# Windowed attention: the mask added by a matmul, maxima of two heads at once, exponentials read from PSUM

## What is computed

```python
def local_attention(q, k, v):
    w = n // WINDOW                                  # 8 windows
    bq = q.reshape(b, h, w, WINDOW, d) * QK_SCALE    # 8.0
    bk, bv = look_around(bk), look_around(bv)        # the window before and the own one: 256 keys
    sim = jnp.einsum('bhwid,bhwjd->bhwij', bq, bk)
    mask = (i < j) | (i > j + WINDOW) | (j == -1)
    sim = jnp.where(mask, -jnp.finfo(sim.dtype).max, sim)
    attn = jax.nn.softmax(sim, axis=-1)
    out = jnp.einsum('bhwij,bhwjd->bhwid', attn, bv)
```

## Time and profile before

| | |
|---|---|
| median of 3 runs | 1829.39 us (1828.5 to 1833.63) |
| the profiled execution | 1827.51 us, span 1825.5 us |
| TensorE busy | 1616.9 us (89%) |
| VectorE busy | 1272.9 us (70%) |
| ScalarE busy | 862.0 us (47%) |
| GpSimd busy | 425.2 us (23%) |
| mean granted TensorE clock | 0.938 of full speed |

### The profile page before, as it was taken

How to read it: one execution, slowest core, us unless ns; L and a number is a source line. 1 busy time by engine, 2 the same in 40 slices (tenths; PEclk the granted TensorE clock), 3 DMA queues, 4 the chain that set the end, 5 groups by cost and what they waited for, 6 DMA issues and landing times. The chain is left out here.

```text
span 1825.5 us, 27251 instructions
## 1 busy us (share of the span) xinstructions
PE 1616.9 (89%) x8733; PEld 1025.5 (56%) x8733; DVE 1272.9 (70%) x2366; ACT 862.0 (47%) x1584; POOL 425.2 (23%) x258
## 2 busy tenths in 40 slices
PE   6899999999987989898986898898699888888698
PEld 2512222222234878787874765775477765665476
DVE  3588988888876565757574683693777693693776
ACT  3305666666632514242422673674533674574442
POOL 2130000000015020202022372272322372263133
PEclk8958999999989989898988999999799999999799
DMA  5812222222200330303005000000100200000010
GB/s 179 152 18 36 36 36 36 37 36 36 36 21 20 97 116 0 115 0 115 0 0 195 28 2 1 0 0 0 46 1 14 61 2 1 0 0 0 23 47 23
DMA packets 59892, 71.56 MB, mean 39 GB/s; under 512 B 15234, under 2 KB 43794, under 8 KB 59796
## 3 DMA queue, kind: packets, MB, share of 16 engines
q1 hardware_dynamic: 58708, 66.98, 15.3%
q10 hardware_dynamic: 1088, 3.41, 0.5%
HBM read 59.66 MB, written 10.49 MB: 38 GB/s over the span
## 5 line engine op out<-in xcount | busy, mean ns | idle before, releaser
L557 DVE TENSOR_REDUCE a_mx<-bank 128x1 f32<-128x512 f32 x592 | 366.8, 685 | 43.5 <-PE bank L608 43.2
L543 ACT ACTIVATE a_pt<-bank 128x1024 f32<-128x1024 f32 x256 | 247.7, 1021 | 173.2 <-PE bank L655 173.2
L608 PE MATMUL bank<-ka,qa 96*128 96x512 bf16 x592 | 219.4, 415 | 5.9 <-PEq L163 2.1
L1803 PE MATMUL bank<-m_hn,m_w 128*128 128x512 f32 x576 | 151.4, 420 | 18.4 <-DVE m_hn L1934 16.4
L1346 PE MATMUL bank<-wqkv,w_hst 128*128 128x512 f32 x576 | 143.0, 411 | 17.3 <-DVE w_hst L1553 17.3
L655 PE MATMUL bank<-qa,ka 99*128 99x512 bf16 x512 | 153.4, 383 | 3.1 <-issue 3.1
L1317 POOL TENSOR_TENSOR w_sm<-w_sm,w_st 128x1024 f32<-128x1024 f32 (+1 forms) x64 | 133.2, 2093 | 86.9 <-DVE w_st L1594 86.9
L608 PEld LDWEIGHTS bank<-ka,qa 96*128 96x128 bf16 x592 | 48.9, 98 | 182.4 <-DVE a_mx L557 144.6
L986 PE MATMUL bank<-f_y,f_ET 128*128 128x256 f32 x768 | 120.8, 308 | 31.2 <-DVE f_y L1091 20.4
L1392 PE MATMUL bank<-w_kT,w_qz 128*128 128x256 f32 (+1 forms) x512 | 127.8, 386 | 18.8 <-DVE w_st L1587 8.8
L1803 PEld LDWEIGHTS bank<-m_hn,m_w 128*128 128x128 f32 x576 | 112.2, 195 | 55.8 <-issue 27.4
(11 more groups left out here) (239 smaller groups left out, 2728.8 us busy)
## 6 DMA issues: line engine op xcount, KB each, us to landing
f_wex<-in_W SPq DMA_DIRECT2D x8, 2048.0 KB, 12.0
qa<-qk_parts SPq DMA_DIRECT2D x66, 128.0 KB, 4.6
ka<-qk_parts SPq DMA_DIRECT2D x66, 128.0 KB, 6.9
qk_parts<-p_parts SPq DMA_DIRECT2D x16, 384.0 KB, 2.6
wqkv_raw<-in_wqkv SPq DMA_DIRECT2D x2, 1536.0 KB, 8.5
w<-in_w SPq DMA_DIRECT2D x2, 1536.0 KB, 8.7
phi<-in_phi SPq DMA_DIRECT2D x5, 512.0 KB, 3.6
p_xT<-in_xT ACTq DMA_DIRECT2D x2, 1024.0 KB, 9.9
```

Source lines behind the costliest of these rows:

```text
L543: nc.scalar.activation(pt[n % 2][:, 2 * ab:2 * ab + 2, :].rearrange("p h t -> p (h t)"), PB[ab][:, :], ACT.Exp, scale=HD0 ** -0.5).then_in ...
L557: V.reduce_max(mx[par][:, u // 2, u % 2:u % 2 + 1], mbank(u), X).then_inc(max_done, 1)
L608: mm(mbank(u), qa[slot][0:KS, h, it * P:(it + 1) * P], ka[slot][0:KS, h, jh * HALF:(jh + 1) * HALF], start=True, stop=True).then_inc(max_p ...
L1803: last = mm(PB[2 + f % 2][:, part * HALF:(part + 1) * HALF], w1s[cw][:, k, col + f * P:col + (f + 1) * P], hns[ch][:, hf, k, :], start=(n ...
```

## The change

The mask and the identity are kept in bf16 as well; GpSimd makes the copies. A matmul of the bf16 identity with the mask, broadcast over two heads, writes the mask into the PSUM of a pair of heads, and the two score matmuls add to it. The factor 8 goes into the copy of the queries. VectorE takes the negated maximum of two heads in one instruction that reads PSUM alone. The exponentials read the scores from PSUM and write sm. Semaphores count pairs: `s_ps`, `s_max` (in place of `s_masked`) and `e_done`. TensorE now waits for `e_done` where it waited for `s_masked`, and for `zeroed` at 6 instead of 4 a layer.

```diff
+        maskb, identb = sb("maskb", [P, 2 * WIN], BF16), sb("identb", [P, P], BF16)
...
+        def pair_of_heads(w, h):
+
+            c0 = (h % 4) * 2 * WIN
+            return PB[1 + h // 4][:, c0:c0 + 4 * WIN].rearrange("p (e n) -> p e n", e=2)[:, :, keys(w)]
...
-                pool.wait_ge(zeroed, 4 * (l + 1))
+                pool.wait_ge(zeroed, 6 * l + 4)
                 pool.wait_ge(ld_tab, 16 * 4 * (l + 1))
                 pool.wait_ge(G["ld_tab"], 32)
+                V.tensor_copy(maskb[:, :], mask[:, :]).then_inc(zeroed, 1)
+                V.tensor_copy(identb[:, :], ident[:, :]).then_inc(zeroed, 1)
...
                 pe.wait_ge(G["wqkv_high"], KD * (l + 1))
-                pe.wait_ge(zeroed, 4 * (l + 1))
+                pe.wait_ge(zeroed, 6 * (l + 1))
...
                         for h in heads:
-                            if h % 2 == 0 and w >= 1:
-                                pe.wait_ge(s_masked, H1 * (NW * b + w - 1) + h + 2)
+                            n = keys(w).stop - keys(w).start
+                            if h % 2 == 0:
+                                if w >= 1:
+                                    pe.wait_ge(e_done, HP * (NW * b + w - 1) + h // 2 + 1)
+                                mm(pair_of_heads(w, h), identb[:, :], maskb[:, keys(w)].unsqueeze(1).to_broadcast([P, 2, n]),
+                                   start=True, stop=False)
                             c0 = (h % 4) * 2 * WIN + keys(w).start
-                            n = keys(w).stop - keys(w).start
-                            mm(PB[1 + h // 4][:, c0:c0 + n], qz[:, w % 2, h // 2, h % 2, :],
-                               kT[:, h // 2, k0:k0 + n], start=True, stop=True).then_inc(s_ps, 1)
+                            last = mm(PB[1 + h // 4][:, c0:c0 + n], qz[:, w % 2, h // 2, h % 2, :],
+                                      kT[:, h // 2, k0:k0 + n], start=False, stop=(h % 2 == 1))
+                            if h % 2 == 1:
+                                last.then_inc(s_ps, 1)
...
-                            pe.wait_ge(s_masked, H1 * (NW * b + min(i, NW)))
+                            pe.wait_ge(e_done, HP * (NW * b + min(i, NW)))
...
                         for h in hs:
+                            if h == 0 and w >= 2:
+                                act.wait_ge(pt_ps, HP * (NW * b + w - 1))
                             if h % 2 == 0:
-                                act.wait_ge(s_masked, H1 * (NW * b + w) + h + 2)
-                            last = S(sm[:, w % 2, h, keys(w)], sm[:, w % 2, h, keys(w)], ACT.Exp,
-                                     bias=st[:, w % 2, 1, h:h + 1], scale=-1.0, accum_out=st[:, w % 2, 2, h:h + 1])
-                            if h % 4 == 3:
+                                act.wait_ge(s_max, HP * (NW * b + w) + h // 2 + 1)
+                            last = S(sm[:, w % 2, h, keys(w)], pair_of_heads(w, h - h % 2)[:, h % 2, :], ACT.Exp,
+                                     bias=st[:, w % 2, 1, h:h + 1], accum_out=st[:, w % 2, 2, h:h + 1])
+                            if h % 2 == 1:
                                 last.then_inc(e_done, 1)
...
-                                     PB[0][64 * e:64 * e + 64, 0:HALF].rearrange("p (a t) -> p a t", a=HP), ACT.Copy)
+                                     PB[0][64 * e:64 * e + 64, 0:HALF].rearrange("p (a t) -> p a t", a=HP), ACT.Copy,
+                                     scale=QK_SCALE)
...
                     def maxima(w, heads):
-                        s = w % 2
-                        if w >= 2:
-                            dve.wait_ge(pt_ps, HP * (NW * b + w - 1))
                         for h in heads:
-                            if h % 2 == 0:
-                                dve.wait_ge(s_ps, H1 * (NW * b + w) + h + 2)
-                                dve.sem_inc(passed, 1)
-                            c0 = (h % 4) * 2 * WIN
-                            V.tensor_tensor_reduce(sm[:, s, h, keys(w)], PB[1 + h // 4][:, c0:c0 + 2 * WIN][:, keys(w)],
-                                                   mask[:, keys(w)], -QK_SCALE, HIGHEST, ALU.add, ALU.min,
-                                                   st[:, s, 1, h:h + 1]).then_inc(s_masked, 1)
+                            dve.wait_ge(s_ps, HP * (NW * b + w) + h // 2 + 1)
+                            dve.sem_inc(passed, 1)
+                            if h == 0 and w >= 2:
+                                dve.wait_ge(e_done, HP * (NW * b + w - 1))
+                            V.tensor_reduce(st[:, w % 2, 1, h:h + 2], pair_of_heads(w, h), X, ALU.max,
+                                            negate=True).then_inc(s_max, 1)
```

More of the change, by code:

```diff
@@ L1265, in stage_attention1 @@
             "ld_tab", "tabs", "zeroed", "h_high", "h_low", "qk_ps", "v_ps", "qk_sb", "v_sb", "sq_done", "ss_done", "n_sqrt", "n_step"))
-        (qn_done, cos_done, sin_done, turn_done, tq_ps, tk_ps, qz_done, kT_done, s_ps, s_masked, e_done,
+        (qn_done, cos_done, sin_done, turn_done, tq_ps, tk_ps, qz_done, kT_done, s_ps, s_max, e_done,
          d_done, p_done, pt_ps, pt_act, pt_dve, pv_ps, oT_done, wo_ps, wo_done) = (sem(n) for n in (
-            "qn_done", "cos_done", "sin_done", "turn_done", "tq_ps", "tk_ps", "qz_done", "kT_done", "s_ps", "s_masked",
+            "qn_done", "cos_done", "sin_done", "turn_done", "tq_ps", "tk_ps", "qz_done", "kT_done", "s_ps", "s_max",
             "e_done", "d_done", "p_done", "pt_ps", "pt_act", "pt_dve", "pv_ps", "oT_done", "wo_ps", "wo_done"))
@@ L1578, in maxima @@
                     def maxima(w, heads):
-                        s = w % 2
-                        if w >= 2:
-                            dve.wait_ge(pt_ps, HP * (NW * b + w - 1))
                         for h in heads:
-                            if h % 2 == 0:
-                                dve.wait_ge(s_ps, H1 * (NW * b + w) + h + 2)
-                                dve.sem_inc(passed, 1)
-                            c0 = (h % 4) * 2 * WIN
-                            V.tensor_tensor_reduce(sm[:, s, h, keys(w)], PB[1 + h // 4][:, c0:c0 + 2 * WIN][:, keys(w)],
-                                                   mask[:, keys(w)], -QK_SCALE, HIGHEST, ALU.add, ALU.min,
-                                                   st[:, s, 1, h:h + 1]).then_inc(s_masked, 1)
+                            dve.wait_ge(s_ps, HP * (NW * b + w) + h // 2 + 1)
[4 more added lines that the diff above has]
+                                            negate=True).then_inc(s_max, 1)
                     def inverse_sums(w, j):
                         hs = slice(4 * j, 4 * j + 4)
-                        dve.wait_ge(e_done, 2 * (NW * b + w) + j + 1)
+                        dve.wait_ge(e_done, HP * (NW * b + w) + 2 * j + 2)
                         V.reciprocal(st[:, w % 2, 3, hs], st[:, w % 2, 2, hs]).then_inc(d_done, 1)
@@ L1629, in _ @@
                         if 1 <= i <= NW:
-                            maxima(i - 1, range(2))
+                            maxima(i - 1, (0,))
                         if i >= 2:
@@ L1633, in _ @@
                         if 1 <= i <= NW:
-                            maxima(i - 1, range(2, H1 - 2))
+                            maxima(i - 1, (2, 4))
                         if i >= 2:
@@ L1645, in _ @@
                         if 1 <= i <= NW:
-                            maxima(i - 1, range(H1 - 2, H1))
+                            maxima(i - 1, (6,))
                         if i < NW - 2:
```

## The result

The changed kernel takes 1841.77 us (median of 7 executions, 1839.83 to 1847.83) against 1828.5 us (7 executions, 1827.47 to 1833.63) before: a ratio of 1.0078, 95% interval 1.0059 to 1.0097. It is slower, by 13 to 14 us. The forecast was slower, 1855.7 us with a range from 1841 to 1868: the sign is right, the loss is half of what I worked out, and the time is at the range's lower edge.

What follows compares the result with a forecast made beforehand. TensorE was taken to bound projections and the stretch behind the steady windows, VectorE the ramp. Terms 8.7 + 6.3 + 7.9 + 5.6 - 2.0 - 0.2 gave +26.3 us: 1855.7 us, range 1841 to 1868.

Steps and rivals of the forecast that it cites:

- start of both layers: TensorE's layer start waits for GpSimd's mask and identity copies, made after the tables land: +4.3 and +4.4 us.
- output projection: Mid-kernel projection (i = 6) waits for the last pair's exponentials instead of the maxima: 1.6 us later, four runs, +6.3 us.
- masks behind the steady windows: Nine mask matmuls of 0.22 us where TensorE alone is the limit: 2.0 us a run, +7.9 us in all.
- masks in the steady windows: Sixteen masks add 3.5 us, TensorE's free 2.13 us absorb part: 1.4 us a run, +5.6 us in all.
- exponentials at the four waits: ScalarE's exponentials read PSUM, some 0.03 us less each; hidden except where the last is waited for: -0.2 us.
- VectorE in the ramp: Before and just behind the steady windows' start, about six cheaper maxima pairs save 0.5 us a run: -2.0 us.
- windows that stay at 9.54 us: Sign that the prediction is wrong; it expected the steady window to lengthen from 9.54 to about 9.9 us.
- rival (a): Masks cost nothing, slipping into TensorE's gaps; only the waits are left: +12.8 us, 1842 us. Chance 0.13.
- rival (b): A mask costs 0.38 us because switching between fp32 and bf16 breaks the overlap: +15.6 us more, 1871 us. Chance 0.10.
- (c): The 1.6 us wait before the output projection lets TensorE's clock fall, four times: +12 us, 1867 us. Chance 0.07.
- (d): Faster: GpSimd's probabilities shrink 1.0 us without the old maxima, and masks are hidden: -15 us, 1814 us. Chance 0.04.
- (e): The new waits are shorter than thought and part of the masks is hidden: +5 us or less. Chance 0.05.

Runs made afterwards that it cites:

- its experiment: Changed kernel, but the output projection waits only for the exponentials of heads 0 to 3, whose PSUM it overwrites: 1835.27 us, ratio 1.0035 to the kernel before.

## Why the prediction was right in sign and twice too large

Lengths in the traces, all four runs of the body together, beside my terms:

| term | forecast | measured | from |
|---|---|---|---|
| start of both layers | +8.7 | +10.0 | 8.10 and 8.01 against 3.05 us |
| output projection | +6.3 | +6.4 | 1.61 us idle each; 6.5 by its experiment |
| masks behind the steady windows | +7.9 | +7.0 | 1.75 us each; 7.0 by leaving them out |
| masks in the steady windows | +5.6 | 0 | window 9.54 us with and without |
| exponentials at the four waits | -0.2 | -0.5 | eighth turn to last addition 47.76 against 44.52 us, less 1.61 and 1.75 |
| VectorE in the ramp | -2.0 | -1.9 | first to eighth turn 0.66, 0.85 and 0.61 us shorter in the first, second and fourth run, 0.22 longer in the third |
| end of VectorE's loop, twice | not seen | -4.6 | 0.17 and 0.18 against 2.51 and 2.48 us |

Together +16.4 us, against my +26.3. TensorE's four projections took 1.0 us less in the trace than before (142.03 against 143.05 us), and what lies outside the attention 0.2 more; this makes the 15.6 us by which the two profiled executions differ from the first layer's start on. The medians differ by 13.3 us. The 2.3 us between these lie between executions of the same kernel, and no trace shows where.

**Right.** The two new waits, their places and their prices; with 10.0 and 6.4 us they are as large as the whole sum. For the layer start I had 4.3 us and it is 5.0: the casts took the 0.6 us forecast, but I let TensorE start right at the end of the last cast, and it comes another 0.73 us after it (1006.41 to 1007.14), and 0.72 in the second layer, as it did behind the memset before. The price of a mask (0.22 us at three of four places), the reduce (starts 0.60 us apart, 1095.39 and then the reciprocal at 1095.99) and the exponential (L1483 498 ns before at 256 columns, now 0.47 us) are as forecast. GpSimd was not relieved: its two probabilities take 4.73 us together in the loop as before.

**Wrong: the free time of TensorE in the steady windows.** The step was "only 2.13 us are free", the difference of length and busy time in the earlier trace rows, of which I let 16 masks exceed 1.4 us a run. The rows show 0.77 us free in each window, 3.1 in four, and a set of masks took 0.77 us and not 0.88. The busy time was too high by 0.22 us a window: 0.17 is the tail of the matmuls ahead of the wait, counted to their modelled end, and 0.05 is the slower start behind it. By my own sign, windows that stay at 9.54 us, this part of the prediction was wrong. It makes 5.6 of the 10.7 us between my sum and the traces.

**Not seen: the length of a loop's body.** I counted the maxima's instructions only by their durations. Removing instructions also shortened the body that VectorE goes back to, and its return now comes without a load of instructions, which is worth 2.3 us each time. It was in the trace of before as an idle time of 2.51 us put down to "issue", ahead of VectorE's first instruction of the second batch. This makes another 4.6 us.

**Luck.** My terms' own bounds gave +19 to +34 us, and +13.3 lies outside them. The time fell into the range by 0.8 us only because rival (a) had set its lower edge. That rival's 1842 us were met almost exactly, but not by its mechanism: the masks cost 7.0 us behind the steady windows, and a gain at the loop's end that it did not know made up for most of it. Two of my sums were off by rounding: by their terms the layer starts are 4.2 and 4.3 us, and rival (b) adds 16.0 us.

**Rivals.** (a) is right for the steady windows and refuted behind them. (b) is out: a mask among fp32 matmuls is followed after 0.22 us, and costs no more. (c), a fall of the clock at the projection, is out in all four runs of the trace: from the eighth turn to the last addition, with the projection in it, they take 47.76, 47.76, 47.76 and 47.75 us. (d) is out by GpSimd's unchanged 4.73 us. (e) is out: both waits came in full.

**What stays open.** The clock's part. Behind the loop's ends the projections take, in the trace of the changed kernel (length, TensorE busy, granted clock, DMA):
```profile
1148.85:1184.26 35.41, 35.41 (x144) 0.95 0.00 0
1573.23:1607.10 33.87, 33.87 (x144) 1.00 0.00 0
```
The first spends two of its first microseconds (1150 to 1152) at a granted clock of 0.50, the lower of the two levels (1.2 GHz); the second never falls, though TensorE had been idle for 2.23 and 2.24 us ahead of them. Before the change they took 35.81 and 35.27 us, at 0.94 and 0.96 and behind 4.57 and 4.54 us of idle time. And the one long window of the third run, 10.22 us, lies where the granted clock was 0.76 for 5 us. I can't say how much of the 13 us is such chance. Nor was the limit of the loop's length measured, nor what else decides near it.

## What to carry to other kernels

Two waits cost what the change itself would not have: ask of each wait that an edit moves to a later semaphore, what stands in front of that semaphore on its engine, and wait only for the part that the memory in question needs. Work moved to a nearly full engine was free up to a sharp limit, and the idle time placed this limit too early (0.55 us for 0.77); one run with the work doubled finds it, and the rows around the wait say the same. A change that takes work from a relieved engine to the bounding one pays only in the stages where the bound is another, so it is worth making it stage by stage: masks on TensorE in the steady windows, on VectorE in the last two, was the fastest version here.

## What the hardware showed unasked

A return to the start of VectorE's long loop body costs 2.45 to 2.65 us of standing still, a shorter body 0.16 to 0.18. Each of the five long returns in the ten traces has a packet of 8 KB on the DMA queue for instructions, none of the fifteen short ones has. 68 one-column memsets brought the gap back in one of two layers, 136 in both, while 34 of them run in 0.5 us.

TensorE's start of a layer came 0.72 or 0.73 us after the last of GpSimd's memsets or casts that it waits for, in four starts of the traces before and after the change.

A bf16 mask of 512 columns among fp32 scores took 0.22 us, but only 0.12 behind the weighted sums, where the scores that follow took 0.97 us to the next row without it and 0.86 with it.
